# Mamba layer: the input projection divided in three over different states, the gate's half five states later, the closing behind the third scan

## The chip, the cores and the metric

The program runs on one core of a Trainium2 chip. The metric is the device time of one execution in microseconds. The program has twelve parts (eight network layers and what connects them); the change lies in one, the Mamba layer (`mamba`), for 16 sequences of 256 tokens with 128 features.

## The reference, cut to what matters

```python
xn = _layernorm(x, ln_gamma, ln_beta)
proj = xn @ W_in + b_in                      # 128 -> 512
u, res = jnp.split(proj, 2, axis=-1)         # 256 for u, 256 for the gate
up = jnp.pad(u, ((0, 0), (k - 1, 0), (0, 0)))
u = sum((up[:, i:i + seq, :] * conv_w[i] for i in range(k))) + conv_b    # k = 4
u = jax.nn.silu(u)
dt, Bm, Cm = jnp.split(u @ W_x, [DT_RANK, DT_RANK + N_STATE], axis=-1)   # 64, 16, 16
delta = jax.nn.softplus(dt @ W_dt + b_dt)
A = -jnp.exp(A_log)
# per time step: h = exp(dt*A)*h + (dt*u)*B ; y = sum over 16 states of h*C
y = _selective_scan(u, delta, A, Bm, Cm, D)  # + u*D
y = y * jax.nn.silu(res)
return y @ W_out + b_out + x
```

## The kernel before, in words

**Tiling.** Channels lie on the 128 partitions, so the 256 inner channels are two blocks (`ND` = 2), c = 0 and 1, side by side in tiles of 128 x 2 x 256 tokens. Each engine has its own program, and between them stand only semaphores. The loop body (`dve_body`, `act_body`, `pe_body`) is one sequence s: 16 states n, one scan each. POOL has a flat loop over sequences and states.

**The states.** For a state n, POOL makes `w` from `duT` and a column of `bT` (`pool_inputs`); TensorE transposes it into a PSUM bank (`pe_inputs`, two states ahead of the scan); ScalarE makes the decay `dA` from `delta` (`act_decay`, four states ahead, n=0 of the next sequence at n=12); VectorE scans (`dve_scan`). Every two states VectorE multiplies the states by C (`dve_read`, group n/2), and TensorE adds them up in bank `YB` (`pe_sum`) and broadcasts the next C (`pe_broadcast`).

**The preparation of the next sequence** runs in stages, spread over the states of the running one. Which stage runs behind which state is written by hand in `DVE_WHEN`, `ACT_WHEN`, `PE_WHEN`. Stage 0 transposes the normalised tokens to `xT`. Stage 1 on TensorE is the whole input projection: for u, per block, four shifted products (the convolution folded into the weights) and a small edge correction into bank `UB`, and for the gate one product per block into bank `RB`. ScalarE adds biases (`cv` for u, `rs` for the gate). SiLU is x times exp(-ln(1+exp(-x))): stage 2 is the first exponential of `e1` (u) and `e2` (gate), stage 3 their logarithms and second exponentials, each pair behind one table load. Stage 4 on VectorE multiplies `uc` = cv*e1 and `gr` = rs*e2; TensorE projects `uc` (L2486), ScalarE copies it out (`xd`, `top`). Stage 5 is `rest` on VectorE, `mid` and `z` on ScalarE, the product for `z` on TensorE; stage 7 is `bc` and a transposition. Stage 6 is the softplus: `az` = |z|, exponential, logarithm (ScalarE), then `delta` and delta*u (VectorE) and their transposition, which stage 8 copies to `duT` for POOL.

**The end of the previous sequence** runs in the same body: at `FINISH` VectorE closes y (`dve_finish`: adds u*D, two instructions, and multiplies by the gate `gr`), at `OUT` TensorE projects it into `RB` (`pe_out`), at `IN_PLACE` ScalarE scales x in place (`act_residual`, signal `x0_ready`), at `RESIDUAL` VectorE adds `RB` to x (`dve_residual`, waits for `o_psum` and `x0_ready`), and statistics follow in the three states behind it.

**Order.** An engine executes its queue in written order; a waiting instruction holds up all behind it. Within a state VectorE's order is: scan, read, closing or residual or statistics, preparation. ScalarE's: decay, residual part, preparation. TensorE's: inputs, sum and broadcast, out-projection, preparation. Both kernels have `IN_PLACE` = 5: ScalarE's residual part stands behind the decay of state 9.

Of the kernel before, what the change touches and what calls it, by code (L numbers as in the profile page):

```python
# [13 lines left out]
ALU = mybir.AluOpType  # L14
# [4 lines left out]
P = 128  # L19
# [2269 lines left out]
def mamba(nc, g):  # L2289
# [41 lines left out]
    names = ["xn", "xTp", "xT", "urp", "ub", "e", "e1", "rc", "uc", "xdp", "xd", "dp", "rest", "mid", "bTp", "bT", "bc", "z", "az",  # L2331
             "ez", "lz", "dl", "du", "duTp", "duT", "dA", "w", "dbu", "cp", "hs", "hc", "y", "yy", "op", "x0", "x",
             "st", "mv", "mvs"]
    (xn_ready, xT_psum, xT_ready, ur_psum, ub_ready, e_ready, e1_ready, rc_ready, uc_ready, xd_psum, xd_ready, d_psum,
# [42 lines left out]
    def dve_prepare(dve, s, k, stage):  # L2377
        if stage == 4:
            dve.wait_ge(rc_ready, s + 1)
            if not (isinstance(s, int) and s < 2):  # L2380
                dve.wait_ge(o_psum, s - 1)
            dve.tensor_tensor(uc[k][:, :, :], cv[:, :, :], e1[:, :, :], ALU.mult)
            dve.tensor_tensor(gr[k][:, :, :], rs[:, :, :], e2[:, :, :], ALU.mult).then_inc(uc_ready, 1)
# [30 lines left out]
    def act_prepare(act, s, k, stage):  # L2414
# [3 lines left out]
        if stage == 1:  # L2418
            act.wait_ge(ur_psum, s + 1)
            for c in range(ND):  # L2420
                act.activation(cv[:, c, :], UB[:, c * 256:(c + 1) * 256], ACT.Identity, bias=conv_all[:, c:c + 1])
# [3 lines left out]
            ins.then_inc(ub_ready, 1)  # L2425
        if stage == 2:
            act.wait_ge(ub_ready, s + 1)
            act.activation(e1[:, :, :], cv[:, :, :], ACT.Exp, scale=-1.0)
            act.activation(e2[:, :, :], rs[:, :, :], ACT.Exp, scale=-1.0).then_inc(e_ready, 1)
        if stage == 3:  # L2430
            act.wait_ge(e_ready, s + 1)
            act.activation(e1[:, :, :], e1[:, :, :], ACT.Ln, bias=1.0)
            act.activation(e2[:, :, :], e2[:, :, :], ACT.Ln, bias=1.0).then_inc(e1_ready, 1)
            act.wait_ge(e1_ready, s + 1)
            act.activation(e1[:, :, :], e1[:, :, :], ACT.Exp, scale=-1.0)
            act.activation(e2[:, :, :], e2[:, :, :], ACT.Exp, scale=-1.0).then_inc(rc_ready, 1)
# [11 lines left out]
        if stage == 6:  # L2448
# [7 lines left out]
            act.activation(az[:, :, :], az[:, :, :], ACT.Ln, bias=1.0).then_inc(lz_ready, 1)  # L2456
        if stage == 8:
# [4 lines left out]
    def pe_prepare(pe, s, k, stage):  # L2462
# [7 lines left out]
        if stage == 1:  # L2470
# [3 lines left out]
            for c in range(ND):  # L2474
                for tap in range(4):
                    pe.matmul(UB[:, c * 256:(c + 1) * 256], win4[:, tap, c * P:(c + 1) * P], xT[:, tap:tap + SEQ],
                              start=(tap == 0), stop=False)
                pe.matmul(UB[:, c * 256:c * 256 + 3], g.ident[:, :], edge[:, c, 0:3], start=False, stop=True)
# [3 lines left out]
            ins.then_inc(ur_psum, 1)  # L2482
# [44 lines left out]
    def dve_finish(dve, s, k):  # L2527
# [5 lines left out]
        dve.wait_ge(yy_ready, s * 2 + 1)  # L2533
        dve.tensor_tensor(yy[k][:, :, :], yy[k][:, :, :], gr[k][:, :, :], ALU.mult).then_inc(yy_ready, 1)
# [82 lines left out]
    DVE_WHEN = {6: 4, 8: 5, 9: 7, 10: 6}  # L2617
    ACT_WHEN = {1: (0,), 2: (1,), 3: (2,), 4: (3,), 7: (4,), 8: (5, 6), 11: (8,)}
    PE_WHEN = {0: (0,), 1: (1,), 6: (4,), 7: (5,), 8: (7,), 11: (6,)}
    FINISH, OUT, IN_PLACE, RESIDUAL = 1, 3, 5, 7  # L2620
# [13 lines left out]
    def dve_start(dve):  # L2634
        for stage in (4, 5, 7, 6):
            dve_prepare(dve, 0, 0, stage)
        dve_norm(dve, 1)

    def dve_body(dve, s, k, nxt):
        for n in range(NS):  # L2640
            dve_scan(dve, s, n)
            if n % 2 == 0 and n:
# [14 lines left out]
            if nxt is not None and n in DVE_WHEN:  # L2657
                dve_prepare(dve, nxt, 1 - k, DVE_WHEN[n])
# [334 lines left out]
```

## Time and profile before

| | |
|---|---|
| median of 3 runs | 3591.49 us (3590.48 to 3598.76) |
| the profiled execution | 3603.78 us, span 3601.9 us |
| its mean granted TensorE clock | 0.841 |
| busy, share of the span: TensorE, VectorE, ScalarE, POOL | 70%, 60%, 36%, 32% |
| Mamba scans (L2513) | 256, mean 1209 ns |
| Mamba layer | about 2494 to 3160 us of the span |

Busy shares are over the whole program. A stretch of the Mamba layer is read by itself. In the timeline a row is a run of like instructions: its start, how long until the last of them ends, their number, and in brackets the idle time of that engine ahead of it with what ended it. On VectorE and ScalarE the next instruction starts a little before the last one's end, so what an instruction costs is the distance of two starts. PE is TensorE's matmul, PEld its weight load, DVE VectorE, ACT ScalarE. One fp32 matmul or transposition can show as two records.

### The profile page before, as it was taken

The numbers are of one execution on the slowest core, as the hardware profiler recorded it, in microseconds if no ns is written. First come the engines' busy times: TensorE is split into PE (matmuls) and PEld (weight loads), VectorE is DVE, ScalarE is ACT, GpSimd is POOL, SyncE is SP. The second block draws the span as 40 slices with busy tenths as digits, with TensorE's granted clock in tenths as the row PEclk, the third lists the DMA queues.
The fourth block names the chain that finished last, engine by engine and source line by source line (L and its number), as shares of the span: only waits on it lengthen the run. The fifth ranks groups of instructions, "written<-read, shape, count | busy, mean of one in ns | idle before, by whom it ended". The sixth has DMA issues, their size and how long they took to land. (4 is left out here: it accounts for less than half of the span.)

```text
span 3601.9 us, 45275 instructions
## 1 busy us (share of the span) xinstructions
PE 2536.2 (70%) x13811; PEld 1690.7 (47%) x13811; DVE 2161.0 (60%) x5963; ACT 1291.0 (36%) x2797; POOL 1162.6 (32%) x1205
## 2 busy tenths in 40 slices
PE   2899999999997444663392899765788888851090
PEld 0565655655655432452271555454555555540070
DVE  3666666666665449653015666475788888837016
ACT  1343343343341420131130445432767767610040
POOL 2223132132130000004452111101777777710641
PEclk9999999999999765695695888877899999955595
DMA  7100000000001000000123222200000000000112
GB/s 229 43 1 1 0 0 0 0 0 0 0 0 37 16 0 0 0 0 20 52 64 88 71 70 74 84 0 0 1 0 0 0 0 0 0 0 1 53 59 75
DMA packets 105738, 94.08 MB, mean 26 GB/s; under 512 B 12252, under 2 KB 92022, under 8 KB 105462
## 3 DMA queue, kind: packets, MB, share of 16 engines
q1 hardware_dynamic: 97942, 76.97, 7.6%
q0 software_dynamic: 7680, 15.81, 1.3%
q8 instruction: 42, 0.69, 0.1%
q14 instruction: 74, 0.61, 0.1%
HBM read 62.27 MB, written 46.26 MB: 30 GB/s over the span
## 5 line engine op out<-in xcount | busy, mean ns | idle before, releaser
L2572 POOL TENSOR_SCALAR mb_w<-mb_duT,mb_bT 128x256 f32<-128x256 f32 x512 | 473.8, 948 | 141.2 <-PE bank L2582 141.0
L2513 DVE TENSOR_TENSOR_SCAN mb_hs<-mb_dA,bank 128x512 f32<-128x512 f32 x256 | 305.4, 1209 | 46.4 <-PE bank L2582 42.0
L618 POOL TENSOR_TENSOR e_w<-e_w,gla_az 128x2048 f32<-128x2048 f32 x16 | 72.3, 4522 | 653.5 <-ACT gla_az L389 653.5
L2601 PE MATMUL bank<-mb_hc,ident 128*128 128x512 f32 x512 | 249.4, 610 | 23.1 <-DVE mb_hc L2523 23.1
L509 DVE TENSOR_TENSOR gla_qm<-bank,gla_ex 64x256 f32<-64x256 f32 x256 | 107.8, 421 | 204.5 <-ACT gla_en L495 202.7
L1877 DVE TENSOR_REDUCE ra_mx<-bank 128x2 f32<-128x512 f32 x256 | 167.1, 687 | 101.8 <-PE bank L1754 99.8
L2563 ACT ACTIVATE mb_dA<-mb_delta,mb_A 128x255 f32<-128x255 f32 x512 | 218.5, 497 | 10.7 <-DVE mb_hs L2513 10.5
L500 ACT ACTIVATE gla_s<-bank 128x256 f32<-128x256 f32 x128 | 49.2, 384 | 438.3 <-DVE gla_s L521 437.3
L446 PE MATMUL bank<-c_gate_sums,e_w 128*128 128x384 f32 x512 | 191.9, 499 | 0.0
L1963 ACT ACTIVATE ra_pT<-bank 128x512 f32<-128x512 f32 x256 | 139.7, 595 | 132.6 <-PE bank L1774 131.3
L2582 PE MATMUL bank<-ident,mb_w 128*128 128x128 f32 x1024 | 150.6, 278 | 40.4 <-DVE mb_hs L2513 31.0
L494 ACT ACTIVATE gla_ex<-bank 128x384 f32<-128x384 f32 x256 | 126.1, 493 | 123.5 <-PE bank L446 123.4
L1528 ACT ACTIVATE e_hid<-bank,e_b 128x512 f32<-128x512 f32 (+1 forms) x128 | 81.2, 634 | 237.7 <-PE bank L1547 234.7
L1539 PE MATMUL bank<-ident,e_x 128*128 128x128 f32 x112 | 18.8, 292 | 199.4 <-DMA e_x<-queue 199.4
L38 POOL TENSOR_TENSOR scrap<-ones 128x1 f32<-128x1 f32 x96 | 19.9, 207 | 422.8 <-DVE ra_qk L1871 261.3
L1511 POOL DMA_INDIRECT results<-e_y,e_x x112 | 107.2, 957 | 147.5 <-DVE e_y L1582 122.5
L2523 DVE TENSOR_TENSOR mb_hc<-mb_hs,bank 128x1024 f32<-128x1024 f32 x128 | 152.8, 1194 | 0.0
L2582 PEld LDWEIGHTS bank<-ident,mb_w 128*128 128x128 f32 x1024 | 116.7, 142 | 64.0 <-issue 49.4
L408 DVE TENSOR_REDUCE gla_ss<-gla_sq 128x8 f32<-128x512 f32 x128 | 87.3, 682 | 91.7 <-ACT gla_sq L386 91.7
L2601 PEld LDWEIGHTS bank<-mb_hc,ident 128*128 128x128 f32 x512 | 87.2, 190 | 101.3 <-issue 61.5
L1576 DVE COPY e_xT<-bank 128x512 f32<-128x512 f32 (+1 forms) x32 | 19.7, 616 | 188.8 <-PE bank L1539 188.7
L456 PE MATMUL bank<-gla_qm,gla_km 128*128 128x256 f32 x512 | 131.5, 379 | 2.1 <-ACT gla_s L500 2.1
(509 smaller groups left out, 6663.9 us busy)
## 6 DMA issues: line engine op xcount, KB each, us to landing
results<-const_empty SPq DMA_DIRECT2D x2, 4096.0 KB
e_got<-results SPq DMA_DIRECT2D x32, 256.0 KB, 3.4
rope_rows<-ra_part SPq DMA_DIRECT2D x48, 128.0 KB, 1.9
ra_k<-rope_rows SPq DMA_DIRECT2D x32, 192.0 KB, 3.2
ra_q<-rope_rows SPq DMA_DIRECT2D x32, 192.0 KB, 4.2
queue<-const_spare_rows SPq DMA_DIRECT2D x1, 4128.0 KB
e_x<-queue SPq DMA_DIRECT2D x8, 516.0 KB, 4.5
e_w<-in_L_ffn_w SPq DMA_DIRECT2D x2, 2048.0 KB, 8.1
```

Of the source, the lines that this page charges most:

```text
L446: ins = pe.matmul(EX[t][:, 0:3 * P], lna[k][:, t, ch], g.gate_sums[:, t, :], start=True, stop=True)
L456: pe.matmul(SC[t][:, 0:256], km[b][:, t, :], qm[b][:, t, :, :].rearrange("p h t -> p (h t)"), start=True, stop=True)
L494: act.activation(ex[b][:, t, :], EX[t][:, 0:3 * P], ACT.Exp)
L509: dve.tensor_tensor(qm[b][r, :, hd, :], q[r, :, :], e[r, :, 0:P], ALU.mult)
L1877: dve.tensor_reduce(mx[:, :, a, p], halves(MX[a]), AXX, ALU.max).then_inc(mx_ready, 1)
L1963: act.activation(pT[p % 4][a][:, :, :], halves(SB[a]), ACT.Exp, scale=SC).then_inc(p_ready, 1)
L2513: dve.tensor_tensor_scan(hs[n // 2 % 2][:, n % 2, :, :].rearrange("p c t -> p (c t)"), dA[n % RD][:, :, :].rearrange("p c t -> p (c t)"), ...
L2523: dve.tensor_tensor(hc[grp % 2][:, :, :, :], hs[grp % 2][:, :, :, :], RC[grp % 2][:, :].rearrange("p (n t) -> p n t", n=2).unsqueeze(2) .b ...
L2563: ins = act.activation(dA[n % RD][:, c, 1:SEQ], delta[k][:, c, 1:SEQ], ACT.Exp, scale=A[:, c, n:n + 1])
L2572: ins = pool.tensor_scalar(w[n % RH][:, h, :], duT[k][:, h, :], bT[k][:, h, n:n + 1], None, ALU.mult)
L2582: ins = pe.transpose(DB[n % 2][:, c * 256 + h * P:c * 256 + (h + 1) * P], w[n % RH][:, h, c * P:(c + 1) * P], g.ident[:, :])
L2601: ins = pe.matmul(YB[:, :], g.ident[:, :], hc[grp % 2][:, j, :, :].rearrange("p c t -> p (c t)"), start=(n == 0), stop=(n == NS - 1))
```

## The change

The projection is divided: on TensorE stage 1 now is block 0 of u at state 1, a new stage 2 is block 1 of u at state 2 (behind the sum and broadcast of that state), and a new stage 9 is the gate at state 7, behind the product for `z`. Before stage 9 TensorE waits until the previous sequence's residual has read `RB`. ScalarE takes `cv` and the first exponential of `e1` at state 3, the logarithm and second exponential at state 4, the gate's bias and first exponential at state 8 behind `z`, and the gate's logarithm and second exponential at the end of stage 6 (state 9). VectorE multiplies `uc` at state 6 and `gr` at state 12. `FINISH` goes from 1 to 2 and, within the state, ahead of the read; `OUT` from 3 to 4; `RESIDUAL` from 7 to 6, which puts it and the statistics one state earlier, the residual ahead of `uc`. The closing waits in addition for `gr`, and `pe_out` for the gate of the following sequence to be copied out of `RB`. In the prologue of sequence 0 the same stages run in a row. New semaphores `r_psum`, `r_ready`, `er_ready`, `lr_ready`, `e2_ready`, `gr_ready` order them (their declaration is left out below).

```diff
@@ -2379,8 +2380,10 @@
             dve.wait_ge(rc_ready, s + 1)
             if not (isinstance(s, int) and s < 2):
                 dve.wait_ge(o_psum, s - 1)
-            dve.tensor_tensor(uc[k][:, :, :], cv[:, :, :], e1[:, :, :], ALU.mult)
-            dve.tensor_tensor(gr[k][:, :, :], rs[:, :, :], e2[:, :, :], ALU.mult).then_inc(uc_ready, 1)
+            dve.tensor_tensor(uc[k][:, :, :], cv[:, :, :], e1[:, :, :], ALU.mult).then_inc(uc_ready, 1)
+        if stage == 9:
+            dve.wait_ge(e2_ready, s + 1)
+            dve.tensor_tensor(gr[k][:, :, :], rs[:, :, :], e2[:, :, :], ALU.mult).then_inc(gr_ready, 1)
         if stage == 5:
             dve.wait_ge(xd_ready, s + 1)
             dve.scalar_tensor_tensor(out=rest[:, :], in0=top[:, :], scalar=g.part_signs[:, 0:1], in1=TB[:, 256:512],
@@ -2418,22 +2421,24 @@
         if stage == 1:
             act.wait_ge(ur_psum, s + 1)
             for c in range(ND):
-                act.activation(cv[:, c, :], UB[:, c * 256:(c + 1) * 256], ACT.Identity, bias=conv_all[:, c:c + 1])
+                ins = act.activation(cv[:, c, :], UB[:, c * 256:(c + 1) * 256], ACT.Identity, bias=conv_all[:, c:c + 1])
+            ins.then_inc(ub_ready, 1)
+        if stage == 2:
+            act.wait_ge(ub_ready, s + 1)
+            act.activation(e1[:, :, :], cv[:, :, :], ACT.Exp, scale=-1.0).then_inc(e_ready, 1)
+        if stage == 3:
+            act.wait_ge(e_ready, s + 1)
+            act.activation(e1[:, :, :], e1[:, :, :], ACT.Ln, bias=1.0).then_inc(e1_ready, 1)
+            act.wait_ge(e1_ready, s + 1)
+            act.activation(e1[:, :, :], e1[:, :, :], ACT.Exp, scale=-1.0).then_inc(rc_ready, 1)
+        if stage == 9:
+            act.wait_ge(r_psum, s + 1)
             for c in range(ND):
                 ins = act.activation(rs[:, c, :], RB[:, c * 256:(c + 1) * 256], ACT.Identity,
                                      bias=bin_[:, 2 + c:3 + c])
-            ins.then_inc(ub_ready, 1)
-        if stage == 2:
-            act.wait_ge(ub_ready, s + 1)
-            act.activation(e1[:, :, :], cv[:, :, :], ACT.Exp, scale=-1.0)
-            act.activation(e2[:, :, :], rs[:, :, :], ACT.Exp, scale=-1.0).then_inc(e_ready, 1)
-        if stage == 3:
-            act.wait_ge(e_ready, s + 1)
-            act.activation(e1[:, :, :], e1[:, :, :], ACT.Ln, bias=1.0)
-            act.activation(e2[:, :, :], e2[:, :, :], ACT.Ln, bias=1.0).then_inc(e1_ready, 1)
-            act.wait_ge(e1_ready, s + 1)
-            act.activation(e1[:, :, :], e1[:, :, :], ACT.Exp, scale=-1.0)
-            act.activation(e2[:, :, :], e2[:, :, :], ACT.Exp, scale=-1.0).then_inc(rc_ready, 1)
+            ins.then_inc(r_ready, 1)
+            act.wait_ge(r_ready, s + 1)
+            act.activation(e2[:, :, :], rs[:, :, :], ACT.Exp, scale=-1.0).then_inc(er_ready, 1)
         if stage == 4:
             act.wait_ge(xd_psum, s + 1)
             act.activation(xd[:, :], TB[:, 256:512], ACT.Copy)
@@ -2454,6 +2459,10 @@
             act.activation(bT[k][:, :, :], halves(TB[:, 0:256])[:, :, P - NS:P], ACT.Copy).then_inc(bT_ready, 1)
             act.wait_ge(ez_ready, s + 1)
             act.activation(az[:, :, :], az[:, :, :], ACT.Ln, bias=1.0).then_inc(lz_ready, 1)
+            act.wait_ge(er_ready, s + 1)
+            act.activation(e2[:, :, :], e2[:, :, :], ACT.Ln, bias=1.0).then_inc(lr_ready, 1)
+            act.wait_ge(lr_ready, s + 1)
+            act.activation(e2[:, :, :], e2[:, :, :], ACT.Exp, scale=-1.0).then_inc(e2_ready, 1)
         if stage == 8:
             act.wait_ge(duT_psum, s + 1)
             act.activation(duT[k][:, :, :], TB[:, :].rearrange("p (h d) -> p h d", h=2), ACT.Copy)\
@@ -2471,15 +2480,19 @@
             pe.wait_ge(xT_ready, s + 1)
             if not first(s):
                 pe.wait_ge(z_ready, s)
-            for c in range(ND):
-                for tap in range(4):
-                    pe.matmul(UB[:, c * 256:(c + 1) * 256], win4[:, tap, c * P:(c + 1) * P], xT[:, tap:tap + SEQ],
-                              start=(tap == 0), stop=False)
-                pe.matmul(UB[:, c * 256:c * 256 + 3], g.ident[:, :], edge[:, c, 0:3], start=False, stop=True)
+        if stage in (1, 2):
+            c = stage - 1
+            for tap in range(4):
+                pe.matmul(UB[:, c * 256:(c + 1) * 256], win4[:, tap, c * P:(c + 1) * P], xT[:, tap:tap + SEQ],
+                          start=(tap == 0), stop=False)
+            ins = pe.matmul(UB[:, c * 256:c * 256 + 3], g.ident[:, :], edge[:, c, 0:3], start=False, stop=True)
+            if c == ND - 1:
+                ins.then_inc(ur_psum, 1)
+        if stage == 9:
             for c in range(ND):
                 ins = pe.matmul(RB[:, c * 256:(c + 1) * 256], win[:, DI + c * P:DI + (c + 1) * P], xT[:, 3:3 + SEQ],
                                 start=True, stop=True)
-            ins.then_inc(ur_psum, 1)
+            ins.then_inc(r_psum, 1)
         if stage == 4:
             pe.wait_ge(uc_ready, s + 1)
             for c in range(ND):
@@ -2531,6 +2544,7 @@
                                            in1=YB[:, c * 256:(c + 1) * 256], op0=ALU.mult, op1=ALU.add)
         ins.then_inc(yy_ready, 1)
         dve.wait_ge(yy_ready, s * 2 + 1)
+        dve.wait_ge(gr_ready, s + 1)
         dve.tensor_tensor(yy[k][:, :, :], yy[k][:, :, :], gr[k][:, :, :], ALU.mult).then_inc(yy_ready, 1)
 
     def dve_residual(dve, s):
@@ -2602,10 +2616,10 @@
                             start=(n == 0), stop=(n == NS - 1))
         ins.then_inc(y_psum, 1)
 
-    def pe_out(pe, s, k, more):
+    def pe_out(pe, s, k):
         pe.wait_ge(yy_ready, s * 2 + 2)
-        if more:
-            pe.wait_ge(ub_ready, s + 3)
+        if not (isinstance(s, int) and s == NSEQ - 1):
+            pe.wait_ge(r_ready, s + 2)
         for h in range(2):
             o = RB[:, h * P:(h + 1) * P]
             for c in range(ND):
@@ -2614,10 +2628,10 @@
         ins.then_inc(o_psum, 1)
 
     AHEAD = 4
-    DVE_WHEN = {6: 4, 8: 5, 9: 7, 10: 6}
-    ACT_WHEN = {1: (0,), 2: (1,), 3: (2,), 4: (3,), 7: (4,), 8: (5, 6), 11: (8,)}
-    PE_WHEN = {0: (0,), 1: (1,), 6: (4,), 7: (5,), 8: (7,), 11: (6,)}
-    FINISH, OUT, IN_PLACE, RESIDUAL = 1, 3, 5, 7
+    DVE_WHEN = {6: (4,), 8: (5,), 9: (7,), 10: (6,), 12: (9,)}
+    ACT_WHEN = {1: (0,), 3: (1, 2), 4: (3,), 7: (4,), 8: (5, 9), 9: (6,), 11: (8,)}
+    PE_WHEN = {0: (0,), 1: (1,), 2: (2,), 6: (4,), 7: (5, 9), 8: (7,), 11: (6,)}
+    FINISH, OUT, IN_PLACE, RESIDUAL = 2, 4, 5, 6
 
     def turns(start, body, end):
 
@@ -2632,20 +2646,20 @@
         return run
 
     def dve_start(dve):
-        for stage in (4, 5, 7, 6):
+        for stage in (4, 5, 7, 6, 9):
             dve_prepare(dve, 0, 0, stage)
         dve_norm(dve, 1)
 
     def dve_body(dve, s, k, nxt):
         for n in range(NS):
             dve_scan(dve, s, n)
+            if n == FINISH and not first(s):
+                dve_finish(dve, s - 1, 1 - k)
             if n % 2 == 0 and n:
                 dve_read(dve, s, n // 2 - 1)
             elif n == 0 and not first(s):
                 dve_read(dve, s - 1, NS // 2 - 1)
             if not first(s):
-                if n == FINISH:
-                    dve_finish(dve, s - 1, 1 - k)
                 if n == RESIDUAL:
                     dve_residual(dve, s - 1)
                 if n == RESIDUAL + 1:
@@ -2655,7 +2669,8 @@
                 if n == RESIDUAL + 3:
                     dve_keep(dve, s - 1)
             if nxt is not None and n in DVE_WHEN:
-                dve_prepare(dve, nxt, 1 - k, DVE_WHEN[n])
+                for stage in DVE_WHEN[n]:
+                    dve_prepare(dve, nxt, 1 - k, stage)
 
     def dve_end(dve):
         dve_read(dve, NSEQ - 1, NS // 2 - 1)
@@ -2668,7 +2683,7 @@
     def act_start(act):
         act.wait_ge(scales_ready, 1)
         act_tokens(act, 0)
-        for stage in (0, 1, 2, 3, 4, 5, 6, 8):
+        for stage in (0, 1, 2, 3, 4, 5, 9, 6, 8):
             act_prepare(act, 0, 0, stage)
         for n in range(AHEAD):
             act_decay(act, 0, 0, n)
@@ -2692,7 +2707,7 @@
         act_residual(act, NSEQ - 1)
 
     def pe_start(pe):
-        for stage in (0, 1, 4, 5, 7, 6):
+        for stage in (0, 1, 2, 4, 5, 9, 7, 6):
             pe_prepare(pe, 0, 0, stage)
         for grp in range(2):
             pe_broadcast(pe, 0, 0, grp)
@@ -2715,16 +2730,16 @@
                 elif nxt is not None:
                     pe_broadcast(pe, nxt, 1 - k, 0)
             if n == OUT and not first(s):
-                pe_out(pe, s - 1, 1 - k, nxt is not None)
+                pe_out(pe, s - 1, 1 - k)
             if nxt is not None and n in PE_WHEN:
                 for stage in PE_WHEN[n]:
-                    if stage == 1 and not (isinstance(s, int) and s < 2):
-                        pe.wait_ge(x_ready, s - 1)
+                    if stage == 9 and not first(s):
+                        pe.wait_ge(x_ready, s)
                     pe_prepare(pe, nxt, 1 - k, stage)
 
     def pe_end(pe):
         pe_sum(pe, NSEQ - 1, NS // 2 - 1)
-        pe_out(pe, NSEQ - 1, 1, False)
+        pe_out(pe, NSEQ - 1, 1)
 
     def nothing(eng):
         pass
```

## Rows read from the trace of the kernel before

**Rows 1.** Busy time by stretch of one sequence: first and last of 14.
```profile
2562.28:2601.27 38.99, 34.58 (x165) 22.13 (x166) 33.49 (x41) 29.04 (x62) 29.96 (x33) 1.00 0.00 0
...
3069.15:3108.14 38.99, 34.53 (x165) 22.09 (x165) 33.49 (x41) 29.05 (x62) 29.66 (x32) 1.00 0.00 0
```

**Rows 2.** Timeline of VectorE over one sequence: start us, duration us, engine, line, operation.
```profile
3005.08 0.87 DVE L2530 SCALAR_TENSOR_TENSOR mb_uc<-mb_uc,m_D,bank 128x256 f32<-128x256 f32 x2 [0.95 <-PE bank L2601]
...
3007.99 1.19 DVE L2523 TENSOR_TENSOR mb_hc<-mb_hs,bank 128x1024 f32<-128x1024 f32 x1
...
3020.18 0.69 DVE L2382 TENSOR_TENSOR mb_uc<-mb_cv,mb_e 128x512 f32<-128x512 f32 x1 [1.44 <-ACT mb_e L2436]
...
3020.79 0.68 DVE L2383 TENSOR_TENSOR mb_gr<-mb_rs,mb_e 128x512 f32<-128x512 f32 x1
...
3021.39 1.21 DVE L2513 TENSOR_TENSOR_SCAN mb_hs<-mb_dA,bank 128x512 f32<-128x512 f32 x1
...
3025.48 0.47 DVE L2386 SCALAR_TENSOR_TENSOR mb_rest<-mb_top,c_part_signs,bank 128x256 f32<-128x256 bf16 x1
...
3027.00 0.18 DVE L2550 BATCH_NORM_AGGREGATE mb_mv<-mb_st 128x2 f32<-128x6 f32 x1
...
3030.51 0.69 DVE L2394 SCALAR_TENSOR_TENSOR mb_delta<-mb_z,mb_az 128x512 f32<-128x512 f32 x1 [0.49 <-ACT mb_az L2456]
...
3038.55 2.32 DVE L2513 TENSOR_TENSOR_SCAN mb_hs<-mb_dA,bank 128x512 f32<-128x512 f32 x2
```

**Rows 3.** Waits within that sequence: waiting instruction, releaser, total, times, longest (us).
```profile
DVE mb_hs L2513 <- PE bank L2582: 2.5, 2, 1.3
```

**Rows 4.** Timeline of TensorE over the same sequence.
```profile
3006.00 1.97 PE L2476 MATMUL bank<-mb_xT,mb_win 128*128 128x256 f32 x8
...
3007.94 1.98 PE L2476 MATMUL bank<-mb_xT,mb_win 128*128 128x256 f32 x8
...
3010.84 0.60 PE L2582 MATMUL bank<-ident,mb_w 128*128 128x128 f32 x4
...
3011.28 1.88 PE L2601 MATMUL bank<-mb_hc,ident 128*128 128x512 f32 x4
...
3013.65 0.61 PE L2612 MATMUL bank<-W_out,mb_uc 128*128 128x128 f32 x4
```

**Rows 5.** Timeline of ScalarE over the same sequence.
```profile
3011.04 0.84 ACT L2421 ACTIVATE mb_cv<-bank,mb_conv_all 128x256 f32<-128x256 f32 x2 [4.35 <-PE bank L2480]
...
3011.77 0.84 ACT L2423 ACTIVATE mb_rs<-bank,mb_bin 128x256 f32<-128x256 f32 x2
...
3013.28 0.64 ACT L2428 ACTIVATE mb_e<-mb_cv 128x512 f32<-128x512 f32 x1
...
3013.80 0.64 ACT L2429 ACTIVATE mb_e<-mb_rs 128x512 f32<-128x512 f32 x1
...
3015.25 1.28 ACT L2432 ACT_TABLE_LOAD   x1
...
3020.85 0.86 ACT L2411 ACTIVATE x<-x,mb_mrs,mb_rs  x2
...
3025.98 0.42 ACT L2443 ACTIVATE mb_mid<-mb_rest 128x256 bf16<-128x256 f32 x1 [1.34 <-DVE mb_rest L2386]
...
3026.30 0.82 ACT L2446 ACTIVATE mb_z<-bank,b_dt 128x256 f32<-128x256 f32 x2
...
3027.16 0.63 ACT L2450 ACTIVATE mb_az<-mb_z 128x512 f32<-128x512 f32 x1
```

**Rows 6.** TensorE's gaps: steady sequence, last sequence, and busy time with granted clock.
```profile
3033.20 0.63 PE L2582 MATMUL bank<-ident,mb_w 128*128 128x128 f32 x4 [1.09 <-DVE mb_hs L2513]
...
3125.16 0.63 PE L2582 MATMUL bank<-ident,mb_w 128*128 128x128 f32 x4 [2.52 <-DVE mb_hs L2513]
...
3126.18 3.28 PE L2601 MATMUL bank<-mb_hc,ident 128*128 128x512 f32 x4 [0.39 <-DVE mb_hc L2523]
...
3124.00:3128.00 4.00, 2.44 (x7) 1.37 (x8) 4.00 (x4) 1.61 (x4) 4.00 (x5) 0.84 0.01 2
```

More of the change, by code:

```diff
@@ L2330, in mamba @@
     rs12_ready, scales_ready = sig("nrs12"), sig("nscales")
-    names = ["xn", "xTp", "xT", "urp", "ub", "e", "e1", "rc", "uc", "xdp", "xd", "dp", "rest", "mid", "bTp", "bT", "bc", "z", "az",
+    names = ["xn", "xTp", "xT", "urp", "ub", "e", "e1", "rc", "rp", "r", "er", "lr", "e2", "gr", "uc", "xdp", "xd", "dp", "rest", "mid", "bTp", "bT", "bc", "z", "az",
              "ez", "lz", "dl", "du", "duTp", "duT", "dA", "w", "dbu", "cp", "hs", "hc", "y", "yy", "op", "x0", "x",
              "st", "mv", "mvs"]
-    (xn_ready, xT_psum, xT_ready, ur_psum, ub_ready, e_ready, e1_ready, rc_ready, uc_ready, xd_psum, xd_ready, d_psum,
+    (xn_ready, xT_psum, xT_ready, ur_psum, ub_ready, e_ready, e1_ready, rc_ready, r_psum, r_ready, er_ready,
+     lr_ready, e2_ready, gr_ready, uc_ready, xd_psum, xd_ready, d_psum,
      rest_ready, mid_ready, bT_psum, bT_ready, bc_ready, z_ready, az_ready, ez_ready, lz_ready, dl_ready, du_ready, duT_psum, duT_ready,
```

## The prediction

> **What bounds the kernel now.** I first cut the Mamba layer into stretches of one sequence each. The reader is to see fourteen stretches of 38.99 us that agree to a few hundredths in every column, with the TensorE clock at 1.00 throughout [rows 1]. So one sequence can be read for all, and a change of x us in its length is worth 14x: the loop body runs for sequences 0 to 15, and 1 to 14 have both a predecessor to finish and a successor to prepare. No engine fills the stretch: TensorE is busy 34.5 us, VectorE 33.5, POOL 29.7, ScalarE 29.0. What sets the period are handovers between queues that are executed strictly in written order.
>
> Second I read VectorE's part of the timeline of one sequence [rows 2]. I count T from 2999.56, which is one period before the scan of state 15 at 3038.55. VectorE carries the scans, so its stalls are the period's. It stalls 0.95 us ahead of the closing of the previous sequence, 1.44 ahead of `uc`, 0.49 ahead of `delta`, and twice, for 2.5 together, ahead of scans whose inputs TensorE has not transposed [rows 2, 3]. Sum 5.4 us. Third, TensorE's part says why the scans wait: the projection is one unbroken block from 3006.00 to 3010.84, and the inputs of state 4 stand behind it [rows 4]. Fourth, ScalarE's part: `cv` waits 4.35 us for that block, and a serial row of exponential, table load, logarithm, table load, exponential leads to `uc`; then `mid`, `z` and the softplus lead to `delta` [rows 5]. The chain of waits that the page follows back from the end doesn't reach this layer, so it prices nothing here; the timeline does.
>
> **The change, part by part.** No arithmetic is removed or added, and there is no DMA in it. Both kernels switch ScalarE's tables four times a sequence. What changes is order. I walk one steady sequence.
>
> Closing behind the third scan. VectorE was free at 3005.08-0.95 = T 4.57 and now runs scan 2 there (1.11: a pair's 2.32 less a single one's 1.21 [rows 2]) to about 5.7; TensorE's sum was ready at T 5.52. The 0.95 stall is gone. The closing runs to read 0, which before took 7.99-5.08 = 2.91 with a scan in it, now 1.80, so read 0 starts at T 7.5 and is done at 8.7.
>
> The first third (channels 0 to 127 of u) starts as before at T 6.44 and takes 7.94-6.00 = 1.94 [rows 4]. At T 8.38 the inputs of state 4 follow (0.44) and sum 0 at 8.82, which finds read 0 done. Sum and broadcast take 13.65-11.28-0.44 = 1.93, so the second third runs from T 10.75 to 12.69. Inputs 5 stand behind it, done 0.60 later. VectorE has scan 3, 4 and read 1 behind it by T 11.9 and stalls 1.4 for scan 5, in place of the two stalls of 2.5. The out-projection comes behind inputs 6 and sum 1 and is over near T 17.7; nobody needs it before 20.6.
>
> ScalarE to `uc`. Before, `cv` started 0.20 after TensorE went on past the block (3011.04 against 3010.84). Now that is T 12.89, 1.4 later than 11.48, since sum, broadcast and inputs stand inside. From `cv` to the end of the residual's ScalarE part took 3020.85+0.86-3011.04 = 10.67. Of this go: the gate's bias and decay 7, which now comes ahead of `cv`, 13.28-11.77 = 1.51 (0.73 like `cv`'s for the bias, 0.78 for the decay), and the second of three pairs, 3013.80-3013.28 = 0.52 each, 1.56. Added is 0.13 for a wait on `cv` just written (0.86 from `z` to `az` against 0.73 from `cv` to the gate [rows 5]). Left 7.73: the residual's part is over at T 20.62.
>
> The residual's new place. VectorE's residual moves from behind scan 7 to ahead of `uc`, while ScalarE's part, which it waits for, stays at state 5 behind the exponentials. `uc` itself would be ready 0.86+0.78 earlier, yet VectorE is stopped at the residual. It is free from T 16.7 (scans 5 and 6 at 13.3 and 14.4, read 2 at 15.5), so it idles 3.9 us where it idled 1.44. Behind it in the queue are `uc`, scan 7 and everything that prepares the next sequence. From `uc` to `rest` was 5.30 with the gate's product and the residual; without the product (0.60) and with the mean (under 0.2) it is 4.86 from the residual's start. So `rest` starts at 20.65+4.86 = T 25.5, before 25.92. All that the front gained is 0.4 us.
>
> The gate's ScalarE work. `z` starts 0.82 after `rest` as before (26.30-25.48), T 26.35. From `z` to `delta` was 30.51-26.30 = 4.21. Now stage 9 stands in between and one decay with it: 0.73 for the bias, 0.13 for its own wait, 0.52 for the exponential and 0.78 for the decay, while `az` no longer waits for `z`, 0.13 less: 2.03. `delta` starts at T 32.6, before 30.95. VectorE would be there at about T 29.9, so its stall of 0.49 becomes 2.7. Behind it stand scan 11 and the source of the next sequence's `w` on POOL (late by 1.7, less than the period grows). The gate's matmuls behind the second product (about 1 us of TensorE) are covered by that same stall. The gate's logarithm, table load and exponential (0.5+1.3+0.6) come behind `delta` and end near T 35; the product at state 12 is asked for at T 37.3, so only its own 0.60 counts. Were that cover gone, the whole 2.4 would count.
>
> The sum. From `delta` to the scan of state 15 was 38.55-30.51 = 8.04; plus 0.60 it ends at 32.6+8.64 = T 41.25 against 38.99, +2.3 us. The head of the next sequence starts as before, relative to that scan. Stalls tell the same: 5.4 before, 1.4+3.9+2.7 = 8.0 after. Times 14 this is +32 us. The ends: no row shows the new prologue; from the same prices it lies between -3.3 (bias, three second halves and the gate's matmuls of 1 us all saved ahead of `uc`) and +4.4 (2.03 and 2.4 all added behind it). Sequence 0 pays the stage-9 delay, sequence 15 saves the 0.95. I take +1, near the middle. +33 on the profiled execution's 3603.8 (a span of 3601.9 and 1.9 around it) is 3637. The runs' median is 12.3 lower at 3591.5, so the forecast is 3625.
>
> **TensorE's clock.** TensorE's idle 1.09 ahead of inputs 13 grows with VectorE's stall by 2.2, to some 3.2 us. In the last sequence it idled 2.52 ahead of the row at 3125.16; the mean granted clock of that 4 us stretch is 0.84, a mix of 2.4 and 1.2 GHz, and the sum at 3126.18 took 3.28 instead of 1.88 [rows 4, 6]. Behind the new gap lie inputs 14 and sum 5, and inputs 15 behind these. VectorE asks for inputs 15 at T 41.2 and TensorE has them at about 40.0, so of the 1.4 us of a slow sum between 0 and 1.4 reach the period. In the sum I take 0, as the slack of 1.2 nearly holds it. The Trainium skill ("TensorE: Matmul & The Clock Gate", Why this matters for your kernels) states that long idle gaps between bursts of matmuls bring the lower clock back, which speaks against this change; rows 6 agree. By it every sequence would pay, and the sum would be up to 14x1.4 = 20 us longer; by my reading it is not.
>
> **The rivals.**
> The slow clock reaches the path: two transposes, the sum and the broadcast at 1.2 GHz and the return to 2.4 late enough to hold up the scan of state 15. For it: rows 6, and a longer gap than there. Against: the slack. At 0.8 a sequence, between the bounds, 3625+11 = 3636; at 1.4, 3645.
> The gate's half is hidden: stage 9 doesn't lengthen the way to `delta`, because ScalarE takes it while it waits for `mid` (1.34 us idle in the trace). For it: that idle time. Against: stage 9 is written behind `mid` and `z`, and the queue keeps order. Then -2.03x14 = -28, so 3597, no change.
> Faster, one mechanism: ScalarE's results arrive ahead of VectorE's asking. Place: the residual's wait and `delta`'s. ScalarE is idle about 10 us a sequence. If `uc` didn't wait for the residual's part (1.64 less) and `delta`'s 2.7 stall vanished, a period is 41.25-4.3 = 36.9 and the time 3625-4.3x14 = 3564. It decides from the point where the two shrink by more than 2.3 together. Against: ScalarE's idle time lies ahead of `xT`, `cv` and `mid`, all waits for others, and not ahead of these two.
>
> **How the numbers follow.** Forecast 0.56, slow clock 0.20, hidden gate 0.13, faster 0.11. The forecast's own range is 3616 to 3633 (half a microsecond of error a sequence, and the ends). Within 0.3%, or 11 us, a measurement of this kernel can't tell a time from no change. The first two cases are slower by more: 0.76. The range of 0.8 takes in these, with the clock's upper bound, and the edge towards the hidden gate: 3608 to 3645.
>
> **What would show it.** In the changed profile: sequences of 41.2 us; no stall ahead of the closing; one stall of 1.4 ahead of a scan for TensorE; one of about 3.9 ahead of the residual for ScalarE's residual part; `uc` with none; one of about 2.7 ahead of `delta`; the gate's product with none; ScalarE from `z` to `az` 2.9 instead of 0.86. The prediction is wrong if the residual finds its ScalarE part ready, if `delta` is not stalled, or if the clock stands below 1.00 in the steady sequences and scan 15 waits for its inputs.

## The result, and the profile after

The changed kernel takes 3632.6 us (median of 4 runs, 3628.4 to 3635.1), the kernel before 3593.1 beside it: a ratio of 1.0107 with a 95% interval of 1.0089 to 1.0124, +39.5 us. The forecast was 3625, the range 3608 to 3645.

The profiled executions have spans of 3626.6 and 3601.9, which is only 24.7 apart. The Mamba layer alone, from its first normalised token to its last kept statistic, went from 665.9 us (2494.1 to 3160.1) to 703.2 (2484.8 to 3188.0), +37.3. The rest is that this execution reached the layer 9.4 us earlier, and lies in parts that the change doesn't touch. So the layer is read by itself. Busy time by stretch, from one `delta` to the next, for five of the fourteen steady sequences of the changed kernel (stretch, its length, then busy time of TensorE, weight load, VectorE, ScalarE, POOL, and the granted clock):

```profile
2552.93:2594.76 41.83, 34.76 (x164) 21.97 (x164) 33.59 (x42) 29.18 (x62) 29.25 (x32) 1.00 0.00 0
2594.76:2636.58 41.82, 36.02 (x164) 22.84 (x164) 33.58 (x42) 29.18 (x62) 29.25 (x32) 0.96 0.00 1
2719.64:2762.07 42.43, 36.61 (x164) 23.72 (x164) 33.06 (x42) 29.29 (x62) 29.68 (x32) 0.92 0.00 0
...
3012.78:3054.29 41.51, 35.38 (x164) 23.40 (x164) 32.98 (x41) 29.29 (x62) 29.67 (x32) 0.96 0.00 0
3096.65:3138.46 41.81, 35.99 (x164) 22.83 (x164) 33.58 (x42) 29.18 (x62) 29.25 (x32) 0.96 0.00 0
```

Where [rows 1] shows 38.99 throughout, the sequences now take 41.51 to 42.43, 41.82 in the mean. 14 times the difference of 2.83 is 39.6 us; prologue, sequence 0 and sequence 15 together gave 2.3 back, which leaves the layer's 37.3. The fourteen are of three kinds: five take 41.8 us, six 41.5 to 41.6 and three 42.4. The work of VectorE and ScalarE is the same to a few tenths, so what grew is waiting. Timeline of VectorE in the changed kernel, one sequence, against [rows 2]; a scan's releaser reads "issue" where the profile names none:

```profile
3021.43 2.32 DVE L2526 TENSOR_TENSOR_SCAN mb_hs<-mb_dA,bank 128x512 f32<-128x512 f32 x2
...
3027.02 0.84 DVE L2543 SCALAR_TENSOR_TENSOR mb_uc<-mb_uc,m_D,bank 128x256 f32<-128x256 f32 x2
...
3028.53 1.21 DVE L2536 TENSOR_TENSOR mb_hc<-mb_hs,bank 128x1024 f32<-128x1024 f32 x1
...
3034.78 2.33 DVE L2526 TENSOR_TENSOR_SCAN mb_hs<-mb_dA,bank 128x512 f32<-128x512 f32 x2 [1.69 <-issue]
...
3042.20 0.42 DVE L2553 TENSOR_TENSOR x<-bank,x 128x256 f32 x1 [3.97 <-ACT x L2414]
3042.54 0.83 DVE L2383 TENSOR_TENSOR mb_uc<-mb_cv,mb_e 128x512 f32<-128x512 f32 x1
...
3054.29 0.69 DVE L2397 SCALAR_TENSOR_TENSOR mb_delta<-mb_z,mb_az 128x512 f32<-128x512 f32 x1 [2.79 <-ACT mb_az L2461]
...
3058.98 0.69 DVE L2386 TENSOR_TENSOR mb_gr<-mb_rs,mb_e 128x512 f32<-128x512 f32 x1
...
3063.77 2.33 DVE L2526 TENSOR_TENSOR_SCAN mb_hs<-mb_dA,bank 128x512 f32<-128x512 f32 x2 [0.75 <-issue]
```

The closing at 3027.02 and `uc` at 3042.54 start without a stall. The residual waits 3.97 us for ScalarE's residual part, `delta` 2.79 for ScalarE's logarithm, the scan of state 5 1.69 (1.41 in the sequences in which the closing's product takes 1.06 instead of 0.70: the stall takes up the difference). In three of the fourteen sequences the scan of state 15 waits 0.75 to 0.83 as well (last row). ScalarE in the same sequence, against [rows 5]:

```profile
3034.24 0.84 ACT L2424 ACTIVATE mb_cv<-bank,mb_conv_all 128x256 f32<-128x256 f32 x2 [4.89 <-PE bank L2488]
...
3041.12 0.86 ACT L2414 ACTIVATE x<-x,mb_mrs,mb_rs  x2
...
3048.04 0.82 ACT L2451 ACTIVATE mb_z<-bank,b_dt 128x256 f32<-128x256 f32 x2
3048.75 0.84 ACT L2437 ACTIVATE mb_rs<-bank,mb_bin 128x256 f32<-128x256 f32 x2
3049.62 0.63 ACT L2441 ACTIVATE mb_e<-mb_rs 128x512 f32<-128x512 f32 x1
3050.16 0.89 ACT L2577 ACTIVATE mb_dA<-mb_delta,mb_A 128x255 f32<-128x255 f32 x2
3050.96 0.61 ACT L2455 ACTIVATE mb_az<-mb_z 128x512 f32<-128x512 f32 x1
```

From `z` to `az` lie 2.92 us (0.86 before): the gate's bias, its exponential and one decay. TensorE, against [rows 4, 6]: the two thirds of u with a sum between them, and, in another sequence, the gap and what follows it.

```profile
3015.47 1.09 PE L2596 MATMUL bank<-ident,mb_w 128*128 128x128 f32 x4 [3.23 <-DVE mb_hs L2526]
...
3027.81 2.00 PE L2486 MATMUL bank<-mb_xT,mb_win 128*128 128x256 f32 x8
...
3032.19 1.89 PE L2486 MATMUL bank<-mb_xT,mb_win 128*128 128x256 f32 x8
...
2722.33 1.09 PE L2596 MATMUL bank<-ident,mb_w 128*128 128x128 f32 x4 [3.23 <-DVE mb_hs L2526]
...
2724.92 3.52 PE L2615 MATMUL bank<-mb_hc,ident 128*128 128x512 f32 x4
```

The gap ahead of the inputs of state 13 is 3.22 to 3.30 us in all fourteen. In the sequence shown last the transpositions behind it take 1.09 instead of 0.63 and the sum 3.52 instead of 1.88: the lower clock, 1.2 instead of 2.4 GHz. The granted clock falls in thirteen of the fourteen sequences; in the first, behind a gap of 3.30, it stays at 1.00 (the first row above), the transpositions take 0.63 and the sum 1.98. How much of the work behind the gap is slow differs too: the sum takes 3.45 to 3.52 in the three sequences of 42.4 and 1.98 to 3.13 in the others.

### The profile page after: what moved, and what is told of

Same layout as the page of the kernel before. It is cut to its first block and busy times, and to the rows that moved or that the text cites. A ratio compares the mean times of both kernels' runs of the same rounds, so it can differ in the third digit from the quotient of the medians.

```text
span 3626.6 us, 45298 instructions
## 1 busy us (share of the span) xinstructions
PE 2545.0 (70%) x13811; PEld 1700.9 (47%) x13811; DVE 2157.9 (60%) x5963; ACT 1293.7 (36%) x2797; POOL 1159.8 (32%) x1205
## 5 line engine op out<-in xcount | busy, mean ns | idle before, releaser
L2615 PE MATMUL bank<-mb_hc,ident 128*128 128x512 f32 x512 | 258.9, 630 | 16.7 <-DVE mb_hc L2536 16.3
L2596 PE MATMUL bank<-ident,mb_w 128*128 128x128 f32 x1024 | 159.1, 292 | 62.7 <-DVE mb_hs L2526 51.9
L2596 PEld LDWEIGHTS bank<-ident,mb_w 128*128 128x128 f32 x1024 | 124.7, 151 | 82.2 <-issue 67.6
```

The lines of the kernel that those rows point to most:

```text
L2596: ins = pe.transpose(DB[n % 2][:, c * 256 + h * P:c * 256 + (h + 1) * P], w[n % RH][:, h, c * P:(c + 1) * P], g.ident[:, :])
L2615: ins = pe.matmul(YB[:, :], g.ident[:, :], hc[grp % 2][:, j, :, :].rearrange("p c t -> p (c t)"), start=(n == 0), stop=(n == NS - 1))
```

## The experiments

Each is a kernel of its own, timed against the kernel before on the same chip. Beside the time stands the mean length of the fourteen steady sequences from its profile, which is free of what varies in the other layers. For the changed kernel that is 41.82, for the one before 38.99.

**The residual back behind `uc`.**

```diff
-    FINISH, OUT, IN_PLACE, RESIDUAL = 2, 4, 5, 6
+    FINISH, OUT, IN_PLACE, RESIDUAL = 2, 4, 5, 7
```

> The changed kernel with the residual and the statistics back one state later, behind scan 7 and so behind uc (RESIDUAL 6 to 7). Theory (the residual ahead of uc stops VectorE for ScalarE's residual part, and this is on the path): the stall of 3.97 us ahead of the residual goes, VectorE stalls about 2.3 ahead of uc instead, everything behind starts about 1.6 earlier, the sequence falls from 41.8 us (mean of 14) to about 40.2 and the time by about 23 us, to some 3610. Rival (the 3.97 us only replace waiting that would come later anyway, ahead of delta): the stall ahead of delta grows from 2.8 to about 4.4 and the sequence stays at 41.8, the time at 3633.

Measured: 3607.0 us against 3596.1, ratio 1.0028 (1.0017 to 1.0038); sequences 39.70. The stall moved to `uc` and is 2.22, that of `delta` is 2.49. One number, the residual one state late instead of early, takes back 2.1 of the 2.8 us: 1.75 from the stall ahead of `uc` and 0.3 from `delta`'s, which the expectation didn't have. The rival falls.

**ScalarE's residual part at state 2.**

```diff
-    FINISH, OUT, IN_PLACE, RESIDUAL = 2, 4, 5, 6
+    FINISH, OUT, IN_PLACE, RESIDUAL = 2, 4, 2, 6
```

> The changed kernel with ScalarE's residual part at state 2, where ScalarE waits about 5 us for cv, in place of state 5 (IN_PLACE 5 to 2); the residual stays ahead of uc. Theory (what VectorE waits for at the residual is ScalarE's residual part behind the exponentials): the residual finds its part ready, the stall there falls to the out-projection's end (about 1 us or a little more), uc waits for its exponential, together about 2.3 instead of 3.97; ScalarE's copy of the first product comes 0.8 earlier too; the sequence falls by 1.6 to about 40.2, the time to some 3610. Rival (the out-projection, or TensorE, is what ends last there): the stall stays near 4 and the time at 3633.

Measured: 3603.9 against 3596.1, ratio 1.0020 (1.0010 to 1.0029); sequences 39.55. VectorE's timeline at the place of the 3.97 us:

```profile
2863.06 0.42 DVE L2553 TENSOR_TENSOR x<-bank,x 128x256 f32 x1 [0.90 <-PE bank L2627]
2864.37 0.69 DVE L2383 TENSOR_TENSOR mb_uc<-mb_cv,mb_e 128x512 f32<-128x512 f32 x1 [0.89 <-ACT mb_e L2433]
```

The residual can stay ahead of `uc`; what cost was that its ScalarE part stood behind the exponentials. Moved into ScalarE's idle time, it leaves two waits of 0.9, together 1.8 where the expectation had 2.3.

**The gate ahead of stage 5.**

```diff
-    ACT_WHEN = {..., 8: (5, 9), 9: (6,), 11: (8,)}
-    PE_WHEN = {..., 7: (5, 9), 8: (7,), 11: (6,)}
+    ACT_WHEN = {..., 8: (9, 5), 9: (6,), 11: (8,)}
+    PE_WHEN = {..., 7: (9, 5), 8: (7,), 11: (6,)}
```

> The changed kernel with the gate's stage 9 ahead of stage 5 on TensorE (state 7) and on ScalarE (state 8), so that its bias and first exponential run while ScalarE waits 1.67 us for rest. Theory (stage 9 between z and az lengthens the way to delta by 2.0): the stall ahead of delta falls from 2.8 to about 0.8 to 1.0, the sequence from 41.8 to about 40.0 or less, as TensorE's idle stretch and the slow clock behind it shrink too, the time by 25 to 35 us to about 3603. Rival (stage 9 is hidden work, and delta waits for something else, such as the logarithm's table or TensorE's product for z, which now comes 1 us later): the stall stays at 2.8 or grows, and the time is 3633 or more.

Measured: 3615.8 against 3596.1, ratio 1.0048 (1.0031 to 1.0066); sequences 40.38. ScalarE's timeline:

```profile
2915.89 0.63 ACT L2441 ACTIVATE mb_e<-mb_rs 128x512 f32<-128x512 f32 x1
2916.55 0.42 ACT L2448 ACTIVATE mb_mid<-mb_rest 128x256 bf16<-128x256 f32 x1
2916.88 0.82 ACT L2451 ACTIVATE mb_z<-bank,b_dt 128x256 f32<-128x256 f32 x2
2917.59 0.90 ACT L2577 ACTIVATE mb_dA<-mb_delta,mb_A 128x255 f32<-128x255 f32 x2
2918.39 0.62 ACT L2455 ACTIVATE mb_az<-mb_z 128x512 f32<-128x512 f32 x1
```

The gate's two steps are hidden ahead of `mid`, and `delta`'s stall fell from 2.79 to 1.32, not to 0.8 to 1.0. The decay is still between `z` and `az`: the expectation had counted it with stage 9, but it belongs to stage 6's place at state 9. So of the 2.03, stage 9 is 1.41 and the decay the rest.

**Extra matmuls in TensorE's gap.**

```diff
+            if n == 10 and nxt is not None:
+                pe.wait_ge(z_ready, nxt + 1)
+                for _ in range(5):
+                    pe.matmul(UB[:, 0:256], g.ident[:, :], win[:, 0:256], start=True, stop=True)
```

> The changed kernel with five extra matmuls of 128x256 fp32 per sequence on TensorE at the end of state 10, into bank UB, which nobody reads before it is overwritten: about 2.4 us of work in the idle stretch of 3.23 us ahead of the inputs of state 13. Nothing of the computation is changed. Theory (the slow clock behind the idle stretch costs 0.26 to 1.1 us of each sequence, mean 0.6): the granted clock is 1.00 in every sequence, all fourteen take the same, 41.2 to 41.5 us, the stall ahead of scan 15 (0.75 to 0.83 in four sequences) is gone, and the time falls by 4 to 8 us to about 3626. Rival (the clock only slows work that is covered): the clock rises to 1.00 but the time stays within 2 us; or the added work delays inputs 13 and the time rises.

Measured: 3631.3 against 3596.1, ratio 1.0090 (1.0076 to 1.0104). One sequence and all of them, busy time and granted clock:

```profile
2896.64:2938.47 41.83, 36.95 (x176) 23.80 (x175) 33.59 (x42) 29.17 (x62) 29.29 (x32) 1.00 0.00 0
2561.92:3147.65 585.73, 517.54 (x2439) 333.25 (x2438) 470.41 (x574) 408.40 (x855) 410.06 (x448) 1.00 0.00 0
```

The clock is 1.00 and all sequences take 41.83 to 41.85, the mean of the changed kernel; the ratio's interval overlaps that of the changed kernel too. The first rival's forecast of the time holds, its reason only in part, because two effects offset each other. In the changed kernel three of the fourteen sequences (not four, as the expectation has it) take 42.4, with 0.75 to 0.83 of waiting for inputs 15; the extra matmuls take this wait away. But they also lengthen the nine sequences in which the gate's product took 0.69 us: with them it takes 0.92 in all fourteen, as it did before in only the five of 41.8 (why, see the last section). So the slow clock does have a price, about 0.9 us in three sequences against those of 41.5, 0.19 in the mean of fourteen. In the other sequences it costs nothing: 41.51 with the slow clock, and 41.53 at full clock with the same product of 0.69 (the last kernel below). That the two effects cancel is chance.

**The closing back behind scan 1**, with nothing else changed (`FINISH` 2 to 1 in the changed kernel).

> The changed kernel with the closing back behind scan 1 (FINISH 2 to 1). Theory (the closing behind the third scan moves read 0, and with it sum 0 and the second third of the projection, ahead): the 0.95 us stall ahead of the closing comes back, read 0 ends about 0.9 later, sum 0 waits for it, the second third and cv and all behind start about 0.9 later; the sequence rises from 41.8 (mean) to about 42.7 and the time by about 12 us to 3644. Rival (the stall of 1.4 us ahead of scan 5 swallows the closing's wait): the sequence and the time stay as they are.

Measured: 3645.2 against 3603.9, ratio 1.0128 (1.0106 to 1.0150); sequences 42.62, the stall of 0.95 ahead of the closing is back. As expected.

**The kernel before with only the closing moved** (`FINISH` 1 to 2, and `dve_finish` ahead of `dve_read` in `dve_body`).

> The kernel before with only the closing behind the third scan and ahead of the read (FINISH 1 to 2). Theory (in the kernel before TensorE's unbroken block ends what follows, whenever read 0 is done): the 0.95 us stall goes but the stall ahead of scan 4 grows by the same, the sequence stays at 38.99 within 0.1 and the time at 3596. Rival (the closing's wait is worth its 0.95 us by itself): 38.0 a sequence, 14 us less.

Measured: 3601.8 against 3603.9, ratio 0.9998 (0.9986 to 1.0010); sequences 38.98. The stall went to the scan of state 4, whose 1.23 became 2.35:

```profile
2848.17 1.22 DVE L2513 TENSOR_TENSOR_SCAN mb_hs<-mb_dA,bank 128x512 f32<-128x512 f32 x1 [2.35 <-PE bank L2582]
```

The same edit is worth 0.8 us a sequence where a sum waits for read 0, and nothing where the unbroken block stands ahead of the sum. As expected.

**The kernel before with only the projection divided**, in two parts and not in three: the gate stays with block 1 of u, and the out-projection goes one state later.

```diff
-            for c in range(ND):
-                for tap in range(4):
...
+        if stage in (1, 2):
+            c = stage - 1
+            for tap in range(4):
...
+        if stage == 2:
             for c in range(ND):
                 ins = pe.matmul(RB[:, c * 256:(c + 1) * 256], win[:, DI + c * P:DI + (c + 1) * P], xT[:, 3:3 + SEQ],
                                 start=True, stop=True)
...
-    PE_WHEN = {0: (0,), 1: (1,), 6: (4,), ...}
-    FINISH, OUT, IN_PLACE, RESIDUAL = 1, 3, 5, 7
+    PE_WHEN = {0: (0,), 1: (1,), 2: (2,), 6: (4,), ...}
+    FINISH, OUT, IN_PLACE, RESIDUAL = 1, 4, 5, 7
```

> The kernel before with only the projection divided: block 0 of u behind state 1, block 1 of u and the gate together behind state 2 (behind sum 0 and broadcast), the out-projection one state later as in the change; closing, residual and all of ScalarE's order as before. Theory (dividing puts the inputs, a sum and a broadcast inside the chain that leads to cv, and ScalarE's chain to uc and delta is what sets the period): cv comes 3.2 later, of it 0.9 because sum 0 waits for a read 0 that stands behind the closing; uc and all behind come 3.2 later, the sequence is about 42.2 and the time about 3641. Rival (the scans' two stalls of 2.5 us are what the division is worth): the sequence falls by 1 to 2.5, the time to 3561 to 3582.

Measured: 3650.8 against 3603.9, ratio 1.0131 (1.0114 to 1.0148); sequences 42.43. VectorE stalls 5.20 ahead of `uc`, 1.44 before:

```profile
2851.33 0.69 DVE L2382 TENSOR_TENSOR mb_uc<-mb_cv,mb_e 128x512 f32<-128x512 f32 x1 [5.20 <-ACT mb_e L2436]
```

The theory holds (+46.9 us over the kernel before, +45 expected; the sequences 42.43 where it had 42.2), and its rival falls. The division by itself gives the longest time of all these kernels: `uc` waits for a chain that now has inputs, a sum and a broadcast inside.

**All three repairs.** The changed kernel with `IN_PLACE` = 2, stage 9 ahead of stage 5, and stage 6 behind it at state 8 on ScalarE:

```diff
-    ACT_WHEN = {1: (0,), 3: (1, 2), 4: (3,), 7: (4,), 8: (5, 9), 9: (6,), 11: (8,)}
-    PE_WHEN = {0: (0,), 1: (1,), 2: (2,), 6: (4,), 7: (5, 9), 8: (7,), 11: (6,)}
-    FINISH, OUT, IN_PLACE, RESIDUAL = 2, 4, 5, 6
+    ACT_WHEN = {1: (0,), 3: (1, 2), 4: (3,), 7: (4,), 8: (9, 5, 6), 11: (8,)}
+    PE_WHEN = {0: (0,), 1: (1,), 2: (2,), 6: (4,), 7: (9, 5), 8: (7,), 11: (6,)}
+    FINISH, OUT, IN_PLACE, RESIDUAL = 2, 4, 2, 6
```

> The changed kernel with ScalarE's residual part at state 2, the gate's stage 9 ahead of stage 5 on both engines, and stage 6 back to state 8 on ScalarE, so that decay 13 comes behind it as in the kernel before. Theory (the place of the residual part costs 2.2 of the change's 2.8 us a sequence, stage 9 between z and az 1.4, the decay between them 0.65): from the 39.56 measured with the residual part at state 2 the sequence falls by 2.05 to about 37.5, the stall ahead of delta to about 0.7, and the time to about 3575, which is less than the kernel before, so the division itself is sound and the placing was not. Rival (with the two waits gone another engine bounds, TensorE with 34.5 us of work or POOL): 38.5 to 39, about 3590.

Measured: 3570.0 against 3603.9, ratio 0.9916 (0.9898 to 0.9934), faster than both kernels. All sequences take 37.32:

```profile
2816.48:2853.80 37.32, 33.94 (x166) 22.05 (x165) 33.06 (x41) 29.18 (x62) 29.75 (x32) 1.00 0.00 0
```

The theory holds, its rival falls. The clock is at 1.00 with no extra work: the gap ahead of inputs 13 is 1.12 us instead of 3.23, as `delta`'s stall is 0.69 instead of 2.79. What part of the gain over the kernel before is due to the divided projection, and what part to the gate and the residual's ScalarE part in their new places, isn't shown: no run has these places with the projection undivided.

**The same with the residual behind scan 7** (`RESIDUAL` = 7).

> The last kernel (residual part at state 2, gate ahead of stage 5, stage 6 at state 8) with the residual behind scan 7 instead of ahead of uc (RESIDUAL 6 to 7). Theory (two waits stand in a row ahead of uc, the out-projection's and the exponential's, and the residual's own 0.35 us between them): uc starts when its exponential is ready, 0.35 to 0.4 us earlier, and the time falls by about 5 us against that kernel. Rival (the gate on TensorE now waits for the later residual and holds up the product for z behind it): the stall ahead of delta grows, the time is the same or higher.

Measured: 3569.6 against 3603.0, ratio 0.9913 (0.9898 to 0.9929); sequences 37.39, 0.07 longer. The theory fails: `uc` started when its exponential was ready in both kernels, and the residual had stood inside that wait, where it cost nothing. The rival's reason doesn't hold either, as `delta`'s stall went from 0.69 to 0.57; the times of the two kernels are the same within noise.

**Extra matmuls, and the gate's product at state 11** (`DVE_WHEN` 12 to 11 for stage 9); one execution, for its profile.

> The changed kernel with the five extra matmuls (granted clock 1.00 in every sequence) and the gate's product gr at state 11 instead of 12, that is in the stretch in which POOL waits for duT. Read from the profile: with the extra matmuls alone gr took 0.92 us, POOL busy beside it, and the sequence 41.84. Theory (a VectorE product of two SBUF tensors is slower while POOL works): gr takes 0.69 and the sequence 41.84-0.24 = 41.6, if it doesn't wait for its exponential (then up to 0.3 more). Rival (gr's duration has nothing to do with POOL): it stays at 0.92, the sequence at 41.8.

The gate's product over the 16 sequences (shortest, median, longest, in ns), first at state 11, then at state 12 with the same extra matmuls:

```profile
L2386 DVE TENSOR_TENSOR mb_gr<-mb_rs,mb_e x16: 684/688/692, 2515.5 to 3139.6; 128x512 f32<-128x512 f32 x16
```

```profile
L2386 DVE TENSOR_TENSOR mb_gr<-mb_rs,mb_e x16: 691/923/929, 2521.7 to 3152.3; 128x512 f32<-128x512 f32 x16
```

Sequences 41.53 against 41.84. As expected. The sequence falls by more than the product's 0.24, and the closing's product has changed as well, from 1.07 to 0.69.

## Why the prediction was right

Point by point, with T counted from 3021.43, the scan of state 15, as the prediction did.

- **Closing behind the third scan**: forecast without stall at T 5.7, measured 5.59; read 0 7.5 against 7.10 (7.45 in the sequences in which the closing's product takes 1.06 and not 0.70). That the move helps only through sum 0 is shown by the fifth and sixth kernels.
- **Second third, `cv`**: forecast T 12.89, measured 12.81. The stall ahead of scan 5: forecast 1.4, measured 1.41 to 1.71.
- **The residual's place**: ScalarE's part over at 20.62 by forecast, at 3041.12+0.86, T 20.55, in the trace; stall 3.9 against 3.97. It was the largest term, and undoing it in two ways gave 2.1 and 2.3 us a sequence back.
- **The gate's ScalarE work**: `z` to `az` 2.9 against 2.92, `delta`'s stall 2.7 against 2.79, `delta` at T 32.6 against 32.86.
- **The sequence**: forecast 41.25, measured 41.82. The +2.3 was mis-sized by 0.57, a fifth of what came. 0.26 of it is in every sequence (41.51 in the shortest, `delta` at T 32.86 instead of 32.6). The residual started 0.22 after its ScalarE part ended, not 0.03; between the two the trace has VectorE's sequencer working out the address of `x` (64 ns), behind the wait. And `uc` directly behind it cost 3043.30-3042.54 = 0.76 instead of 0.61, since POOL worked beside it, of which below; 0.08 less on the way to `cv` leaves the 0.26. 0.11 is the gate's product, 0.92 instead of 0.69, with what hangs on it, in five of the fourteen. 0.19 is the slow clock in three.
- **The ends**: forecast +1, measured -2.3. This error and that of the sequences have opposite signs, 3.3 us against 8, so the layer's +37.3 lies nearer to the forecast's +33 than the sequences alone would put it. That much is luck.
- **The slow clock**: it was forecast as a rival at 0.8 a sequence and set at 0 in the sum, as the slack of 1.2 would nearly hold a slow sum's 1.4. The clock falls in thirteen of the fourteen sequences. In ten of these the slack holds it, and in three it doesn't: the prediction had named a clock below 1.00 together with a wait of scan 15 for its inputs as a sign of being wrong, and in these three it came true. The slack was right, the slow work wasn't: the transpositions between the gap and the sum are slow as well. At 2722.33 they put the sum 0.45 later, and it takes 3.52 instead of 1.99, so the broadcast behind it starts 2.0 us later after `delta` than with the extra matmuls; less the slack of 1.2 this is about the 0.83 that scan 15 waits. Spread over the fourteen it is 0.19 and not the rival's 0.8. The rule of the Trainium skill ("TensorE: Matmul & The Clock Gate", Why this matters for your kernels) that long idle gaps bring back the lower clock held in thirteen of fourteen; that every sequence would pay for it did not follow, as VectorE waited for TensorE behind the gap in three only.
- "Stalls tell the same" was loose: 5.4 to 8.0 is +2.6, the walk gave +2.3.
- The rivals "hidden gate" and "faster" fell with the two stalls. What the second named as the point of decision was right: with the sequence 4.5 shorter through these two waits, the repaired kernels are faster than the one before.

## What to carry to other kernels

Where several engines run hand-ordered queues, a stall removed is worth only what the next wait behind it leaves: write down, for each moved step, what stands ahead of it on its own queue and when the thing it waits for is done, and walk one period to the end. Moving one half of a handshake (VectorE's residual) without the other (ScalarE's residual part) put an engine's main work behind the tail of another's chain; the same move with both halves, and with new work placed where that engine idles, turned +1.1% into -0.8%. Work in a stall, or a slow clock, costs nothing as long as the slack behind it holds: here 1.2 us of slack held it in ten sequences and fell short by 0.8 in three. An instruction taken out of a stall gains nothing.

## What the hardware showed that was not expected

A VectorE product of two fp32 tensors in SBUF, 128x512, takes 0.69 us alone. The Trainium skill ("GPSIMD Engine Reference", 1. Specifications) lists the SBUF interfaces as shared with VectorE, with contention for instructions with two SBUF inputs. The traces agree, and show how the price is paid: wherever the product and one of POOL's products for `w` (0.92 us alone) ran beside each other from near the start, one of the two paid and the other did not. The gate's product (L2386) and the closing's (L2548), each beside a row of POOL, then `uc`:

```profile
3101.25 0.92 POOL L2586 TENSOR_SCALAR mb_w<-mb_duT,mb_bT 128x256 f32<-128x256 f32 x1 [6.63 <-ACT mb_duT L2468]
3101.34 0.93 DVE L2386 TENSOR_TENSOR mb_gr<-mb_rs,mb_e 128x512 f32<-128x512 f32 x1
...
3112.01 1.06 DVE L2548 TENSOR_TENSOR mb_uc<-mb_uc,mb_gr 128x512 f32<-128x512 f32 x1
3112.03 0.94 POOL L2586 TENSOR_SCALAR mb_w<-mb_duT,mb_bT 128x256 f32<-128x256 f32 x1
...
3027.90 0.70 DVE L2548 TENSOR_TENSOR mb_uc<-mb_uc,mb_gr 128x512 f32<-128x512 f32 x1
3028.03 1.36 POOL L2586 TENSOR_SCALAR mb_w<-mb_duT,mb_bT 128x256 f32<-128x256 f32 x1
...
3042.36 0.93 POOL L2586 TENSOR_SCALAR mb_w<-mb_duT,mb_bT 128x256 f32<-128x256 f32 x1
3042.54 0.83 DVE L2383 TENSOR_TENSOR mb_uc<-mb_cv,mb_e 128x512 f32<-128x512 f32 x1
```

In the first, second and fourth pair VectorE pays: its product ends 0.09 to 0.10 us after POOL's instruction ends, whatever its length, and this is so for all 27 such products longer than 0.73 us in the Mamba layer of the changed kernel. In the third VectorE's product keeps its 0.70, and POOL's takes 1.36. Near a tie either may win: POOL's instruction started 0.02 to 0.05 us after the closing's product and yet won, and in sequence 0 it started 0.03 before `uc` (2541.87) and lost. What decides a tie isn't shown. Put where POOL waits, with none of its work beside it, all 16 of the gate's products took 0.69.

This is also how the slow clock made sequences shorter. Where it had fallen before TensorE transposed delta*u, that took 1.06 us instead of 0.60, POOL had its `duT` later and started its next work in the last third of the gate's product (0.69); where it fell later or not at all (the five of 41.8), POOL worked beside all of it (0.92).
